# Values carried through memory by quarters and turned by VectorE, in place of four TensorE transposes a batch

## What is computed

```python
q = _heads(jnp.concatenate([ssm_states, hidden_states], axis=-1) @ Wq, H)
k, v = _heads(hidden_states @ Wk, HK), _heads(hidden_states @ Wv, HK)
ssm_k, ssm_v = _heads(ssm_states @ Wsk, HK), _heads(ssm_states @ Wsv, HK)
kcat = jnp.concatenate([rep(ssm_k), rep(k)], axis=2)
vcat = jnp.concatenate([rep(ssm_v), rep(v)], axis=2)
scores = q @ kcat / sqrt(D) + alibi          # a key counts for the 64 rows from its own on
o = softmax(where(mask, scores, -inf)) @ vcat @ Wo
x = x + tanh(g_xattn) * o
```

## Time and profile before

| | |
|---|---|
| median of 3 runs | 875.49 us |
| span of the profiled execution, first to last instruction | 871.9 us |
| TensorE (PE) busy | 862.1 us, 99% |
| TensorE weight loads (PEld) busy | 754.0 us, 86% |
| VectorE (DVE) busy | 545.9 us, 63% |
| ScalarE (ACT) busy | 400.6 us, 46% |
| GpSimd (POOL) busy | 519.5 us, 60% |

### The profile page before, as it was taken

The page is one execution under the profiler, slowest core; times in us unless marked ns, Lnnn a source line. Parts: engine busy times, 40 slices in busy tenths (PEclk is TensorE's granted clock), DMA queues, the critical chain, the costliest instruction groups (busy, mean ns, idle before and its releaser), DMA issues.

```text
span 871.9 us, 17392 instructions
## 1 busy us (share of the span) xinstructions
PE 862.1 (99%) x6662; PEld 754.0 (86%) x6662; DVE 545.9 (63%) x983; ACT 400.6 (46%) x810; POOL 519.5 (60%) x532
## 2 busy tenths in 40 slices
PE   9999999999999999999999999999999999999998
PEld 8889999999999999988888868888888888888886
DVE  7675666776666657755436746556655665565567
ACT  5754555554545545654034243444444444444431
POOL 3861443534335232353769998547888888788731
PEclk9999999999999999999999999999999999999999
DMA  8677576776868659630101345311212021121046
GB/s 275 170 142 185 149 200 192 188 197 162 210 164 219 164 138 261 140 98 26 49 24 53 106 147 163 139 50 48 72 50 73 25 72 56 42 73 48 1 137 249
DMA packets 76459, 108.07 MB, mean 124 GB/s; under 512 B 7249, under 2 KB 47954, under 8 KB 75346
## 3 DMA queue, kind: packets, MB, share of 16 engines
q1 hardware_dynamic: 74168, 105.94, 43.2%
q10 hardware_dynamic: 2210, 1.03, 0.4%
HBM read 70.71 MB, written 31.00 MB: 117 GB/s over the span
## 4 chain that ended last, share of the span: by engine, by line
PE 94%; DVE 2%; DMA 1%; issue 1%; ACT 0%; SPq 0%; DVEq 0%; ACTq 0%
PE ps_scores L2219 20%; PE ps_proj L1840 16%; PE ps_scoresT L2219 10%; PE ps_scoresT L1977 7%; PE ps_o L1991 6%; PE ps_proj L1829 6%; PE ps_scores L1950 5%; PE ps_scores L1840 5%; PE ps_proj L2219 5%; PE ps_proj L1898 5%; PE ps_scoresT L1840 4%; DMA xn_rows<-in_x 1%; PE ps_o_max L2018 1%; PE ps_o L1829 1%; PE ps_o_max L1829 1%; PE ps_o_max L1878 1%
## 5 line engine op out<-in xcount | busy, mean ns | idle before, releaser
L1127 ACT ACTIVATE probsT<-ps_scoresT 128x512 f32<-128x512 f32 (+1 forms) x256 | 138.9, 545 | 148.6 <-PE ps_scoresT L1977 144.1
L1485 DVE TENSOR_REDUCE neg_max<-ps_scores 128x2 f32<-128x384 f32 (+1 forms) x256 | 131.7, 517 | 108.1 <-PE ps_scores L1950 107.4
L1352 ACT ACTIVATE part_sums<-ps_scores 128x512 f32<-128x512 f32 x96 | 57.4, 598 | 132.5 <-PE ps_scores L2219 130.5
L1977 PE MATMUL ps_scoresT<-q_stack,k_stack 116*128 116x256 f32 x448 | 106.1, 307 | 0.0
L840 POOL TENSOR_TENSOR o_normal<-o_blocks,inv_sums 128x256 f32<-128x256 f32 x32 | 19.9, 622 | 137.0 <-DVE inv_sums L1506 137.0
L1950 PE MATMUL ps_scores<-k_stack,q_stack 114*128 114x192 f32 (+1 forms) x512 | 94.6, 267 | 2.9 <-DMA q_stack<-qT_hi 1.4
L1950 PEld LDWEIGHTS ps_scores<-k_stack,q_stack 114*128 114x128 f32 x512 | 83.0, 190 | 9.8 <-DMA q_stack<-qT_hi 2.0
L995 POOL TENSOR_TENSOR w_expert_lo<-w_sums,w_expert_hi 128x256 fp32r<-128x256 f32 x64 | 63.8, 1008 | 45.5 <-ACT w_expert_hi L1276 45.5
L1007 POOL TENSOR_TENSOR big<-big,basis 128x512 f32<-128x512 f32 x56 | 77.9, 1409 | 16.3 <-DVE basis L1779 16.3
L1977 PEld LDWEIGHTS ps_scoresT<-q_stack,k_stack 116*128 116x128 f32 x448 | 70.8, 190 | 3.8
L1770 DVE TENSOR_TENSOR basis<-part_sums,silu_gate 128x512 f32<-128x512 f32 x32 | 24.2, 756 | 67.3 <-ACT silu_gate L1360 67.3
(11 more groups left out here) (311 smaller groups left out, 2507.5 us busy)
## 6 DMA issues: line engine op xcount, KB each, us to landing
k_stack<-k_kept SPq DMA_DIRECT2D x64, 192.0 KB, 4.5
big<-coeff_rows SPq DMA_DIRECT2D x8, 1024.0 KB, 4.6
q_stack<-q_kept SPq DMA_DIRECT2D x40, 192.0 KB, 4.1
q_kept<-qT_hi SPq DMA_DIRECT2D x10, 512.0 KB
x_rows<-in_x SPq DMA_DIRECT2D x9, 512.0 KB, 6.6
k_kept<-kT_hi SPq DMA_DIRECT2D x16, 256.0 KB
x_kept<-x_rows SPq DMA_DIRECT2D x16, 256.0 KB, 2.8
w_raw<-in_L_ffn_w_gate SPq DMA_DIRECT2D x16, 256.0 KB, 2.9
```

The lines of the kernel that those rows point to most:

```text
L1127: act.activation(PT[:, g % 2, 2 * j:2 * j + blocks].rearrange("p h f r w -> p (h f r w)"), ST[:, n % 2, 0:blocks].rearrange("p h n -> p (h ...
L1352: act.activation(TP[:, u % 2, j, :], src[:, u % 2, :], ACT.Copy).then_inc(taken, 1)
L1485: dve.tensor_reduce(NM[:, g // 2 % 2, g % 2, 2 * i:2 * i + 2], SA[:, n % 2, :, 0:keys], AX.X, ALU.max, negate=True).then_inc(max_done, 1)
L1977: ins = pe.matmul(ST[:, n % 2, v, :], KS[0:ROWS, g, j + v, 1 - v].rearrange("p w s -> p (w s)"), QS[0:ROWS, g, j + v].rearrange("p f r w - ...
```

## The change

The four transposes of a batch and their PSUM copy go. In their place SyncE stores `vT` to memory in four DMAs, one for each 32 partitions (`keep_v`), and loads it back in one (`load_v`) with quarters of keys on the four groups of 32 partitions. VectorE then turns 32x32 blocks straight into `v_ones`. The copy into `vT` becomes two copies of half the width. Two semaphores are merged into another, one wait of TensorE on the mixture weights goes, and the router's raw weights move to another address with another wait.

```diff
+KEEP_V, LOAD_V = V_PROJ[2] + 2, V_PROJ[2] + 5
...
-        jobs = [("prep", due(n, PREP[t], 2), t) for t in range(TB)] + [("turn_v", due(n, TURN_V), 0)]
+        jobs = [("prep", due(n, PREP[t], 2), t) for t in range(TB)] 
...
-    VT = at("vT", 136 * KIB, [P, 2, NB, W, 2])
+    VT = at("vT", 136 * KIB, [P, 4, NB, W // 4, 2])
+    VQ = at("v_quarters", 138 * KIB, [P, 4, NB, HQ])
...
-    router_raw = at("w_router_raw", 136 * KIB, [P, 4 * P])
+    router_raw = at("w_router_raw", 144 * KIB, [P, 4 * P])
...
+    v_kept_d = nc.dram_tensor("v_kept", (B, 4, HQ, 4, P), F32).ap()
...
+        def keep_v(b):
+            sp.wait_ge(pj_done, passed("v", b, 0))
+            for q in range(4):
+                sp.dma_start(v_kept_d[b, :, :, q].rearrange("k h n -> h k n"),
+                             VT[q * HQ:(q + 1) * HQ].rearrange("p k j w s -> p k (j w s)")).then_inc(v_kept, 16)
+
+        def load_v(b):
+            sp.wait_ge(v_kept, 64 * (b + 1))
+            if b >= 1:
+                sp.wait_ge(v_turned, b)
+            sp.dma_start(VQ[:].rearrange("p q j n -> p (q j n)"),
+                         v_kept_d[b].rearrange("k h q n -> (k h) (q n)")).then_inc(v_in, 16)
...
         keep_k(1)
+        keep_v(0)
+        load_v(0)
         for n in range(SLOTS):
+            b = due(n, KEEP_V, 1)
+            if b is not None:
+                keep_v(b)
+            b = due(n, LOAD_V, 1)
+            if b is not None:
+                load_v(b)
...
             if s == LOAD_ROUTER:
-                sp.wait_ge(v_turned, B - 1)
+                sp.wait_ge(turn_done, passed("prep", B - 1, TB - 1))
...
         def v_out(b):
             dve.wait_ge(v_mm, 2 * (b + 1))
-            dve.tensor_copy(VT[:, b % 2].rearrange("p j w s -> p s (j w)"),
-                            place("v", b, 0).rearrange("p (s n) -> p s n", s=2)).then_inc(pj_done, 1)
+            if b >= 1:
+                dve.wait_ge(v_kept, 64 * b)
+            for s in range(2):
+                ins = dve.tensor_copy(VT[:, :, :, :, s],
+                                      place("v", b, 0)[:, s * T:(s + 1) * T].rearrange("p (j k w) -> p k j w", j=NB, k=4))
+            ins.then_inc(pj_done, 1)
 
         def v_turned_out(b):
-            dve.wait_ge(v_turned, b + 1)
+            dve.wait_ge(v_in, 16 * (b + 1))
             if b == 0:
                 dve.wait_ge(ones_set, 2)
-            dve.tensor_copy(VA[:, :, :, 0:D], turn_place("turn_v", b, 0).rearrange(
-                "p (j g d) -> p j g d", j=NB, g=HK)).then_inc(turn_done, 1)
+            else:
+                dve.wait_ge(pv_mm, HK * b)
+            dve.transpose(VA[:, :, :, 0:D], VQ[:].rearrange("p q j n -> p j q n")).then_inc(v_turned, 1)
...
-        def turn_v(b):
-            dst = take_turn("turn_v", b, 0)
-            pe.wait_ge(pj_done, passed("v", b, 0))
-            for j in range(NB):
-                ins = pe.transpose(dst[:, j * P:(j + 1) * P], VT[:, b % 2, j].rearrange("p w s -> p (w s)"), ident[:])
-            ins.then_inc(v_turned, 1)
...
         def times_v(p):
             b = p // (HK // 2)
-            pe.wait_ge(turn_done, passed("turn_v", b, 0))
+            pe.wait_ge(v_turned, b + 1)
...
-            b = due(n, TURN_V)
-            if b is not None:
-                turn_v(b)
...
-        pe.wait_ge(mix_done, 1)
```

More of the change, by code:

```diff
@@ L332, in build @@
     PC = [POB[:, :, :].rearrange("p h n -> p (h n)"), PNM[:, :, :].rearrange("p h n -> p (h n)")]
-    ident_in, consts_in, gates_in = sem("ident_in"), sem("consts_in"), sem("gates_in")
+    ident_in, consts_in = sem("ident_in"), sem("consts_in")
     ctx_first, ctx_in, x_in, x1_in = sem("ctx_first"), sem("ctx_in"), sem("x_in"), sem("x1_in")
@@ L344, in build @@
     pj_done, turn_done = sem("pj_done"), sem("turn_done")
-    v_turned = sem("v_turned")
+    v_kept, v_in, v_turned = sem("v_kept"), sem("v_in"), sem("v_turned")
     k_kept, q_kept, pad_kept = sem("k_kept"), sem("q_kept"), sem("pad_kept")
@@ L371, in build @@
     xf_in = [sem(f"xf_in{i}") for i in range(PAIRS)]
-    mix_done, c_mm, c_out, c_kept = sem("mix_done"), sem("c_mm"), sem("c_out"), sem("c_kept")
+    c_mm, c_out, c_kept = sem("c_mm"), sem("c_out"), sem("c_kept")
     c_in = [sem("c_in0"), sem("c_in1")]
@@ L673, in _ @@
                                  (escale[:], a["L0_ffn_expert_scale"].rearrange("(e o) -> e o", o=1))):
-                    sp.dma_start(dst, src).then_inc(gates_in, 16)
+                    sp.dma_start(dst, src).then_inc(consts_in, 16)
             b = due(n, KEEP_K, 2)
@@ L1237, in _ @@
             if n == TANH:
-                act.wait_ge(gates_in, 64)
+                act.wait_ge(consts_in, 48 + 64)
                 act.activation(tg[:], gates[:], ACT.Tanh).then_inc(tg_done, 1)
@@ L1649, in mixture @@
         def mixture():
-            dve.wait_ge(gates_in, 64)
+            dve.wait_ge(consts_in, 48 + 64)
             link(dve.tensor_tensor(amp[:], amp[:], amp[:], ALU.mult))
@@ L1655, in mixture @@
             link(dve.reciprocal(mix_sum[:], mix_sum[:]))
-            dve.tensor_scalar(mix[:], amp2[:], mix_sum[:, 0:1], escale[:, 0:1], ALU.mult, ALU.mult).then_inc(mix_done, 1)
+            dve.tensor_scalar(mix[:], amp2[:], mix_sum[:, 0:1], escale[:, 0:1], ALU.mult, ALU.mult)
         def over(v):
```

## The result

| | median | ratio to before | span of the profiled execution |
|---|---|---|---|
| before | 875.35 us (4 runs) | 1 | 871.9 us |
| changed | 883.07 us (4 runs) | 1.0091 (1.0076 to 1.0106) | 880.5 us |

The forecast was 886.4, with a range of 880.5 to 892.5. The way and the mechanism came out as forecast, the loss came out smaller: +7.7 us and not +10.9. In spans of the profiled executions it is +8.6 us: the median stood 3.5 us above that span before, and 2.6 us above it in the changed kernel.

The account below looks back on a forecast made before the run. TensorE was taken as the bound, under way in 862.1 of 871.9 us. Stop +12.2, saving -3.0, loads -0.6 and clock +2.3 gave +10.9 on 875.5: 886.4 us, range 880.5 to 892.5.

Parts of the forecast that it names:

- The wait of batch 0: TensorE stops at scores 23 until VectorE has turned batch 0's values: start 68.4 instead of 56.23, costing 12.2 us.
- the landing of the store: Batch 0's values, queued behind the keys landing at 61.3, take 3.0 us more and reach memory at 64.3.
- the second rival: Batch 0's value stores pass beside the keys, landing at about 61.3; stop 9 to 10 us, about 883 us; chance 0.10.
- The load back: Batch 0's 256 KB of values loaded from memory in 2.8 us, arriving at 67.1.
- The clock: After the stop in batch 0 TensorE restarts at half speed for about 5.7 us, losing 2.3 us.
- The waits given back: Loads awaited before and at batch 1's start gain about 11 us from the stop, so their waits go: -0.6 us.
- The saving: Dropping four transposes a batch frees 0.43 us of TensorE; seven batches count, 3.0 us in all.
- a batch period shorter by 0.43 us: Sign expected on TensorE from batch 2 on, from the transposes' removal.
- VectorE's halves: In slots 20 and 23, two half-width copies and the new transpose add 0.22 us a batch; cost to TensorE 0.
- SyncE in later batches: Five more issues a batch, some 3 us, and a store wait ahead of stacks; 4.9 us of cover, cost 0.
- The third rival: Later batches' stacks come late: five batches lose 1 to 2 us more, about 894 us; chance 0.08.
- The single idle stretch of 11 to 15 us: Sign expected on TensorE's timeline, starting near 56 and released by the maxima of slot 21.

Follow-up runs that it names:

- the filled stop: Changed kernel with 36 float32 matmuls of the identity, results thrown away, put ahead of scores 23 on TensorE: 881.56 us, 1.0084.
- the early trip: Changed kernel with batch 0's four value stores issued ahead of the opening's stacks and their load behind key head 3's stack: 876.43 us, 1.0016.

## Why the prediction was right, and where it was off

**The wait of batch 0, right in place and chain, forecast 3.7 us too long.** Scores 23 were forecast 12.2 us later and came 8.46 us later. SyncE reached the store at 53.76 (54.0 forecast), VectorE turned at 63.48 and TensorE stood from 56.7 to 64.69 behind the maxima of slot 21. The term that was mis-sized is the landing of the store: 64.3 forecast, load issued at 60.61. I had let the values follow the keys, 61.3 plus 3.0, and both parts were too long. By the trace's semaphore events the last of the keys landed at 59.3, 2.0 us sooner than in the kernel before, and the last of the values 1.3 us behind them. The first values had landed at 57.4, so the values did not wait for the last of the keys. From 54 to 59 the DMA engines were busy for a share of 0.70 at 210 GB/s, against 0.54 at 156 GB/s before: the keys' store had left room, and the values' pieces used it. That is the second rival, "the stores pass beside the keys", at 0.10. Its mechanism is what the trace bears out. That its time of 883 came too is in part luck, as it has the saving too high. Why the keys themselves landed sooner is not shown. In the traces with the old order they landed at 60.2, 60.7 and 61.3, so the one trace at hand had given the latest of the three. The load back (2.9 us to VectorE's start, 2.8 forecast) and the last step (1.2 us, 1.27 forecast) were right.

**The clock, right.** Forecast 2.3 us, measured 1.9 by the filled stop. No row before had shown a fall; after it the clock column did, from 59.8 to 70.1 us: half of that idle, half at work. The Trainium skill ("TensorE: Matmul & The Clock Gate", "Why this matters for your kernels") says that a pause between bursts of matmuls drops the clock, and the trace agrees: 0.50 for 10.2 us around the end of a stop of 8.0.

**The waits given back, about right.** Forecast -0.6. With the clock out of it, scores 23 to batch 1 take 10.26 us in place of 10.68: -0.4.

**The saving, wrong by more than half.** Forecast 7 x 0.43 = 3.0 us, measured 1.04 + 0.28 = 1.3. The 0.43 us were read rightly as TensorE's own time: with work in slot 19 the period is 0.44 us shorter, and the same edit gives nothing while the transposes are there. But in batches 1 to 6 the step failed at "what is late next": I named no wait for the exponentials. They showed nothing in the kernel before, because the transposes of slot 19 covered them. Leaving the transposes out alone gives 0.17 us a period, and another 0.28 comes with work put in their place. The sign "a batch period shorter by 0.43 us" was missed for this.

**VectorE's halves, right at 0.** 0.416 us each in place of one of 0.681, and the transposes 0.696 us in place of 0.676. No wait of TensorE in a later batch names them.

**SyncE in later batches, right by luck.** I priced batches 2 to 6, at 0, and they cost 0. I did not price batch 1, where each stack takes four issues. There the five issues, 3.5 us of SyncE's time in the trace of the early trip, cost TensorE a stop of 2.9 to 3.9 us in three kernels, as soon as no long stop in batch 0 hides them. The third rival ("the later stacks come late") was set aside with cover from a batch that has two issues a stack.

Two errors met: the stop 3.7 us too dear, the saving 1.7 us too high. They pull against each other, so half of the first did not show, which is luck. In spans that is +10.9 forecast and +8.6 measured; 883.07 lies inside the range. The single idle stretch of 11 to 15 us that was to show it was 8.0 us long, above the 6 us under which the account would have been wrong.

## What to carry to other kernels

When a step is sent through memory, find the place in the issuing engine's order first: values that lay ready for 30 us were late because their store stood behind others. A wait for one's own store does not belong on an engine with urgent work behind it, whichever engine that is. And a long stop hides others: after it is mended, look again, and fill the slot that lost its work.

## What the runs showed of the hardware

A store of 256 KB issued behind one of 768 KB did not wait until all of that had landed. In 512-byte pieces its first part landed at 57.4 and its last at 60.6, the last of the 768 KB at 59.3. As one DMA in 2 KB rows, issued 3 us sooner, it let the load go out at 60.3. The clock fell to 0.50 at every stop of 2.2 to 8.8 us, between 5.7 us ahead of its end and 1.5 us behind it, for 3.4 to 10.2 us. Shorter waits are not settled: in one run it fell 1.1 us behind a wait of 1.6 us, and in others not behind waits of 1.7 and 1.8 us at the same place, nor behind one of 2.0. In one run it fell with no wait over half a microsecond in the 5 us ahead of it. A store of 256 KB took from a few microseconds in batch 0 to over 12 in batch 7, issued by ScalarE (last issue at 335.75, load issued at 348.15), with the DMA engines full.
